# The second layer's setup: bias products between the weight products, and the second half of the tokens normalised among them

## The reference, cut to what matters

```python
x_ln = layernorm(x, ln_g, ln_b)
q = x_flat @ wq + bq
...
v = interp_flat @ wv + bv
k = interp_flat @ wv + bv
...
qh = heads(q @ mq_w + mq_b)
kh = heads(k @ mk_w + mk_b)
vh = heads(v @ mv_w + mv_b)
...
msa = att @ mo_w + mo_b
z = msa + x.reshape(b, h * w, c)
z_ln = layernorm(z, ln_g, ln_b)
out = gelu(z_ln @ mlp_w + mlp_b) + z
```

## Time and profile before

| | us |
|---|---|
| median of 3 runs | 3997.05 |
| lowest and highest run | 3985.2, 4001.21 |
| profiled execution, its own time | 4001.9 |
| its span, first to last instruction | 4000.0 |
| mean granted TensorE clock | 0.983 of full |

### The profile page before, as it was taken

How to read it: one execution, slowest core, us unless ns; L and a number is a source line. 1 busy time by engine, 2 the same in 40 slices (tenths; PEclk the granted TensorE clock), 3 DMA queues, 4 the chain that set the end, 5 groups by cost and what they waited for, 6 DMA issues and landing times. The chain is left out here.

```text
span 4000.0 us, 63404 instructions
## 1 busy us (share of the span) xinstructions
PE 3823.4 (96%) x21614; PEld 3202.0 (80%) x21614; DVE 2958.2 (74%) x5158; ACT 2430.6 (61%) x5241; POOL 1640.5 (41%) x1935
## 2 busy tenths in 40 slices
PE   8999999999999999999999889999999999999999
PEld 6888888888878888878888657777777777777777
DVE  3984984965957938849849647888787888787876
ACT  3873864855847828738648426565556565555656
POOL 1432432433432333324324215554545454555554
PEclk9999999999999999999999989999999999999999
DMA  2231231331331322313312403131313131313221
GB/s 87 54 77 44 63 78 41 66 91 28 61 83 40 60 71 53 75 43 66 76 43 63 135 26 85 64 85 64 85 64 85 64 85 64 85 64 78 71 73 55
DMA packets 175079, 269.31 MB, mean 67 GB/s; under 512 B 58732, under 2 KB 91560, under 8 KB 174760
## 3 DMA queue, kind: packets, MB, share of 16 engines
q1 hardware_dynamic: 170152, 248.48, 25.0%
q0 software_dynamic: 4608, 16.78, 1.3%
HBM read 113.90 MB, written 33.82 MB: 37 GB/s over the span
## 5 line engine op out<-in xcount | busy, mean ns | idle before, releaser
L647 DVE TENSOR_REDUCE a_neg_max<-a_ps 128x1 f32<-128x1024 f32 x512 | 621.9, 1216 | 303.8 <-PE a_ps L481 303.8
L605 ACT ACTIVATE a_ph<-a_ps 128x512 fp32r<-128x512 f32 x1024 | 564.6, 597 | 190.3 <-PE a_ps L495 188.9
L664 DVE TENSOR_TENSOR a_pl<-a_ps,a_ph 128x512 fp32r<-128x512 f32 x1024 | 654.1, 679 | 7.0 <-ACT a_ph L605 3.7
L749 POOL TENSOR_TENSOR a_qk<-a_fold_s,a_fold_r 64x256 f32<-64x256 f32 x256 | 191.7, 749 | 1039.0 <-DVE a_fold_s L655 864.4
L612 ACT ACTIVATE a_prob<-a_ps,a_neg_max 128x1024 f32<-128x1024 f32 x512 | 572.5, 1118 | 31.2 <-DVE a_neg_max L647 31.2
L495 PE MATMUL a_ps<-a_ident,a_prob 128*128 128x128 f32 x4096 | 553.3, 276 | 37.7 <-DVE a_pl L664 36.6
L495 PEld LDWEIGHTS a_ps<-a_ident,a_prob 128*128 128x128 f32 x4096 | 459.8, 140 | 157.4 <-issue 93.8
L510 PE MATMUL a_ps<-a_ph,a_v 128*128 128x256 f32 x2048 | 550.9, 302 | 0.0
L510 PE MATMUL a_ps<-a_pl,a_v 128*128 128x256 f32 x2048 | 509.9, 282 | 0.0
L481 PE MATMUL a_ps<-a_kl,a_qs 128*128 128x512 f32 x1024 | 404.8, 395 | 0.0
L480 PE MATMUL a_ps<-a_kh,a_qs 128*128 128x512 f32 x1024 | 403.1, 394 | 0.0
(11 more groups left out here) (262 smaller groups left out, 9228.4 us busy)
## 6 DMA issues: line engine op xcount, KB each, us to landing
a_qs<-a_qk SPq DMA_DIRECT2D x128, 256.0 KB, 4.3
a_kl<-a_qk SPq DMA_DIRECT2D x128, 256.0 KB, 4.8
a_xtok<-in_x SPq DMA_DIRECT2D x64, 256.0 KB, 4.9
a_fold_r<-a_inv_row SPq DMA_DIRECT2D x256, 64.0 KB, 3.3
b_xs<-x SPq DMA_DIRECT2D x64, 256.0 KB, 4.6
b_qs<-b_qh SPq DMA_DIRECT2D x64, 256.0 KB, 3.1
b_qs<-b_ql SPq DMA_DIRECT2D x64, 256.0 KB, 3.8
b_z<-x SPq DMA_DIRECT2D x64, 256.0 KB, 3.7
```

Of the source, the lines that this page charges most:

```text
L605: act.activation(ph[:, b % 2, 4 * g:4 * g + 4, (u % 2) * P:(u % 2 + 1) * P], ps[:, 4 + n % 2, :].rearrange("p (k q) -> p k q", k=4), ACT.C ...
L647: dve.tensor_reduce(neg_max[:, i_:i_ + 1], ps[:, 2 * (i_ % 2):2 * (i_ % 2) + 2, :] .rearrange("p a b -> p (a b)"), AX, ALU.max, negate=Tru ...
L664: dve.tensor_tensor(pl[here], ps[:, 4 + n % 2, :].rearrange("p (k q) -> p k q", k=4), raw(ph[here]), ALU.subtract).then_inc(pl_ok, 1)
```

## The change

```diff
-        raws = {n: ... for n in ("mq", "mk", "mv", "mo", "wq", "wv", "mlp")}
+        raws = {n: ... for n in ("mlp", "mk", "mv", "mo", "wq", "wv", "mq")}
...
+            FUSE_BANK = (0, 1, 2, 3, 4, 6, 7)
+            BIAS_AT = (0, 4, 4)
... ACT, in the loop over the 12 products
-                    act.activation(wh[n][:, j, :], ps[:, g % 8, :], ACT.Copy).then_inc(hi_ok, 1)
+                    act.activation(wh[n][:, j, :], ps[:, FUSE_BANK[g % 7], :], ACT.Copy).then_inc(hi_ok, 1)
+                    if g == 5:
+                        for t in range(4, TT):
+                            act.wait_ge(ln_ok, t + 1)
+                            high(act, t).then_inc(xh_ok, 1)
... and behind the loop
-                for t in range(4, TT):
-                    act.wait_ge(ln_ok, t + 1)
-                    high(act, t).then_inc(xh_ok, 1)
... PE
-                    if g >= 8:
-                        pe.wait_ge(lo_ok, g - 7)
+                    if g >= 7:
+                        pe.wait_ge(lo_ok, g - 6)
                     for k in range(CT):
-                        mm = pe.matmul(ps[:, g % 8, :], wt[:, k, j * P:(j + 1) * P], raws[m][:, k, :],
+                        pe.matmul(ps[:, FUSE_BANK[g % 7], :], wt[:, k, j * P:(j + 1) * P], raws[m][:, k, :],
+                                  start=k == 0, stop=k == CT - 1)
+                        mm = pe.matmul(ps[:, 5, g:g + 1], raws[m][:, k, j * P:(j + 1) * P],
+                                       vec[:, BIAS_AT[g // 4] + k:BIAS_AT[g // 4] + k + 1],
                                        start=k == 0, stop=k == CT - 1)
                     mm.then_inc(pe_s, 1)
 
-                pe.wait_ge(lo_ok, 10)
+                pe.wait_ge(lo_ok, 9)
...
                 pe.wait_ge(lo_ok, 12)
-                for g, (at, m) in enumerate(((0, "mq"), (4, "mk"), (4, "mv"))):
-                    for j in range(CT):
-                        for k in range(CT):
-                            mm = pe.matmul(ps[:, 5, 4 * g + j:4 * g + j + 1], raws[m][:, k, j * P:(j + 1) * P],
-                                           vec[:, at + k:at + k + 1], start=k == 0, stop=k == CT - 1)
-                mm.then_inc(pe_s, 1)
... DVE, in the loop over the 12 products
+                    if g == 4:
+                        dve.wait_ge(rstd_ok, 2)
+                        dve.wait_ge(pe_s, 13)
+                        for t in range(4, TT):
+                            prepared(dve, t, t + 1)
+                    if g == 6:
+                        for t in range(4, TT):
+                            dve.wait_ge(xh_ok, t + 1)
+                            low(dve, t).then_inc(xl_ok, 1)
... and at the end of its list
-                dve.wait_ge(rstd_ok, 2)
-                for t in range(4, TT):
-                    prepared(dve, t, t + 1)
-                for t in range(4, TT):
-                    dve.wait_ge(xh_ok, t + 1)
-                    low(dve, t).then_inc(xl_ok, 1)
```

More of the change, by code:

```diff
@@ L924, in layer1 @@
         W = Region(nc, q_at, SB_END)
-        raws = {n: W.take(f"b_{n}_raw", [P, CT, C]) for n in ("mq", "mk", "mv", "mo", "wq", "wv", "mlp")}
+        raws = {n: W.take(f"b_{n}_raw", [P, CT, C]) for n in ("mlp", "mk", "mv", "mo", "wq", "wv", "mq")}
         wqt = W.take("b_wq_t", [P, CT, C])
@@ L1148, in _ @@
                     dve.wait_ge(hi_ok, 1 + g + 1)
-                    dve.tensor_tensor(wl[n][:, j, :], ps[:, g % 8, :], raw(wh[n][:, j, :]), ALU.subtract)\
+                    dve.tensor_tensor(wl[n][:, j, :], ps[:, FUSE_BANK[g % 7], :], raw(wh[n][:, j, :]), ALU.subtract)\
                        .then_inc(lo_ok, 1)
+                    if g == 4:
[7 more added lines that the diff above has]
+                            low(dve, t).then_inc(xl_ok, 1)
                     if g == 3:
@@ L1162, in _ @@
                 dve.tensor_scalar(refs[:], refs[:], -1.0, None, ALU.add).then_inc(chn, 1)
-                dve.wait_ge(pe_s, 22)
+                dve.wait_ge(pe_s, 21)
                 for g, (dst, at) in enumerate(((bqm, 8), (bkm, 12), (bvm, 16))):
@@ L1168, in _ @@
                 dve.tensor_copy(wide[:, 1], vec[:, 36:40].unsqueeze(2).to_broadcast([P, CT, P])).then_inc(chn, 1)
-                dve.wait_ge(pe_s, 23)
+                dve.wait_ge(pe_s, 22)
                 dve.tensor_copy(ref[:], ps[:, 4, :].rearrange("p (c s n) -> p c s n", c=2, s=KT)[:, :, :, 0])\
                    .then_inc(chn, 1)
-                dve.wait_ge(pe_s, 24)
+                dve.wait_ge(pe_s, 23)
                 dve.tensor_tensor(bmo[:], ps[:, 2, :], bo_raw[:], ALU.add).then_inc(chn, 1)
                 dve.tensor_tensor(bmlp[:], ps[:, 3, :], bm_raw[:], ALU.add).then_inc(chn, 1)
-                dve.wait_ge(rstd_ok, 2)
-                for t in range(4, TT):
-                    prepared(dve, t, t + 1)
-                for t in range(4, TT):
-                    dve.wait_ge(xh_ok, t + 1)
-                    low(dve, t).then_inc(xl_ok, 1)
         nc.all_engine_barrier()
```

## The result

| | before | changed |
|---|---|---|
| median, us (7 runs each) | 3998.78 | 3979.94 |
| lowest and highest | 3985.2, 4002.9 | 3974.54, 3985.13 |
| profiled execution, its span | 4001.9, 4000.0 | 3974.67, 3972.9 |

A forecast was written before the change was run, and what follows sets the result against it. PE's list, then DVE's tail, was taken to bound the setup. Savings of 5.2, 0.3, 0.8, 2.1 and 8.2 us sum to 16.6, taking the median from 3997.05 to about 3980.5 us; range 3967 to 3994.

The forecast's parts named there:

- loop, first weight load to the projection's: PE's fused loop with the bias products added: 43.23 us before, plus 11.1, so 54.3 us.
- bias matmul between long ones: In PE's fused loop, each bias matmul pair costs two exposed weight loads: 0.23 us, 11.1 us for 48.
- transposes and wide products to DVE's start: PE behind the projection, now at full clock: transposes 0.7 us to their end, then 7.1; savings 0.8 and 2.1.
- from `b_bmo` to POOL (before 10.10): DVE's tail at the setup's end: the second half of the tokens leaves it, 8.2 us saved.
- block of `centre` and `scale` on DVE: Moved token work, 5.8 us, placed in the fused loop where DVE waited for products, from 2320.8 to 2326.6.
- sum: All setup savings together: bias products 5.2, junction 0.3, transposes 0.8, wide products 2.1, tokens 8.2; -16.6 us.
- two bounds of the prediction: Cost of the bias products in PE's loop: at least 5.5 us (chance 8%), at most 20.5 us (chance 10%).
- 11 us of slack: Before the projection: DVE reaches the low part of g = 8 by about 2336, PE needs it at 2346.9.
- the chain passes beside it, so I give nothing: Behind the barrier: PE's first projection finds a higher clock, but POOL's clearings and DVE's convolution bypass it; no gain.
- the falling clock: In the mixed fused loop, bias matmuls' empty stretches bring PE to 1.2 GHz: loop +49 us, 4029 us, chance 4%.
- the stretch of the first layer with 74 weight loads: Evidence against a clock fall: PE holds 1.00 there with 74 loads in 10 us, most exposed between short matmuls.
- the rival: PE's clock falls to half in the mixed fused loop: 103 us against 54.3, kernel 4029 us, chance 4%.

The follow-up runs named there:

- doubled: Against the changed kernel, each bias matmul issued twice, the second into a spare bank with its result unused: setup 103.89 us, time 3994.99 us.
- The kernel with the bias products alone: Against the changed kernel, the second half of the tokens put back at the end of the setup: setup 101.24 us, ratio to before 0.9983.
- The kernel that clears early: Against the changed kernel, POOL clears `b_qpad` inside the setup, wide products between the projection's halves: first load to first convolution 95.60 us, time 3963.79 us.
- the fourfold one: Against the changed kernel, each bias matmul issued four times throughout the loop: setup 204.21 us, time 4078.84 us.

## Why the prediction was right

By its own steps, from the loop's first weight load on (2292.60 before, 2292.10 in the changed kernel, so its clock times stand 0.5 us early):

| step | predicted | measured |
|---|---|---|
| loop, first weight load to the projection's | 54.3 | 2346.64 - 2292.10 = 54.5 |
| bias matmul between long ones | 0.23 | 0.22 (0.22 when doubled) |
| projection | 11.1 | 11.09 |
| transposes and wide products to DVE's start | 7.8 | 2365.47 - 2357.73 = 7.74 |
| from `b_bmo` to POOL (before 10.10) | 8.2 less | 1.90, 8.2 less |
| block of `centre` and `scale` on DVE | 2320.8 to 2326.6 | 2320.20 to about 2326 |
| low part of g = 8 done | 2336 | 2335.2 |
| sum | -16.6 | -16.39 |

*The dearest unknown was the pair* of weight loads that a bias matmul takes. No row of before had one. The value was built from exposed weight loads: a load hides under a long matmul and not under a one-column one. The loads of the changed kernel show just this, 0.11 us from load to load where no long matmul streams (2298.94 to 2299.05, and again to the second of the two loads in that row) and 0.43 where one does (2299.59 to 2300.02). Two of each make the 1.08. Doubling the matmuls gave the same price again. The two bounds of the prediction, one load a pair (5.5 us) and half clock (20.5 us), were both far off.

*The tokens hid.* Their room was read from the rows as 11 us of slack, and 11.4 is there. The kernel with the bias products alone prices it at 10.11 - 1.90 = 8.2 us, with 8.2 predicted.

*Behind the barrier nothing came back.* PE's first projection there now runs at 1.00 (last window above) and not at 0.50, and clearing to convolution is as long as before. The step "the chain passes beside it, so I give nothing" held. The kernel that clears early shows what that stretch did hide: once the clearings are gone the convolution comes 3.8 us sooner, not 6.8.

*Where the argument was weaker than its result.* Against the falling clock I had put that it "held for 4.5 us of nothing but one-column matmuls". That is thin support: three blocks of 16 such matmuls in this very loop brought it down each time, sooner than in 4.5 us, at 10.2 us for the three. The other support, the stretch of the first layer with 74 weight loads, is no such case: its matmuls have 128 and 256 columns and not one, as in this row:

```profile
1400.93 0.28 PE L510 MATMUL a_ps<-a_ph,a_v 128*128 128x256 f32 x1
```

So the moved products are cheap because each stands between long ones, and not because they are in the loop. The other part of the argument, that each is followed by a long matmul, is the one that carried. What the rival really had to fear I had not named: the mixture has to let the clock rise from the cold start. With one or two bias matmuls a place it rises, with four it doesn't, and at half clock through the loop the rival's own sum, +49 us, would have stood. So a loop of this kind can run at half clock throughout. That one matmul a place is on the safe side had no row behind it, and there the forecast had some luck: the argument for 4% did not reach that far. The rule of the Trainium skill (TensorE: Matmul & The Clock Gate, "A second HAM failure mode: psum-queue depth-cycling") tells of a clock that swings where PE goes round the PSUM banks and pauses shortly between groups of matmuls. The prediction held this rule against the loop, but its condition isn't met here: PE is busy for all of the 49.14 us on seven banks, at 1.00. So no run here shows whether it holds.

*The size in the runs.* The 17.6 us of the ratio, with an interval of 13 to 22, agree with the 16.4 of the setup; nothing more need be explained. In the pair of profiles 0.7 us more is the earlier arrival of `mq`, and 10.2 us lie behind the setup.

## What to carry to other kernels

Spread short matmuls singly among long ones at full clock, and look at what the clock did before and behind every block of them; put no block of short ones among them, not even a filler where the clock has just come up. At the end of a setup, ask of each engine what it still does behind the last wait: here half of the gain was DVE work that had idle room 50 us earlier. A setup of under 3% of the time had 28 us in it (conv 116.41 to 88.32), and the order of loads and the clearings behind the barrier, which no busy share shows, gave nearly two thirds as much as the change did.

## What the runs showed of the hardware that I had not expected

*What the clock does depends on where it starts.* The same mixture (one long fp32 matmul, four of one column) stays at 0.50 when it begins there, for 163 us, and holds 1.00 for 55 us when it begins there. At half clock the mixture also takes 3.41 us a place and at full clock 1.75, so that half as many columns are streamed in a microsecond; whether the clock's earlier level itself matters or only the slower stream that comes of it, these runs don't tell. Each of the two is one execution. Blocks of 16 one-column matmuls, with PE busy throughout, end at half clock (the means of the two shown are 0.81 and 0.78), and some 5 us of long matmuls behind them run at 0.50. Where between two and four a place the mixture no longer rises wasn't tried.

*The scatter of the runs is clock.* The stretch behind the first convolution is the same program in 11 of the 13 profiled executions (in the other two a part of its work has moved ahead of it), and lasts 1591.6 to 1609.0 us. I summed the time at half clock in it, over 160 equal windows, each as 2 x (1 - PEclk) x its length: 33.5 to 67.8 us. Before has 67.8 us of it and lasts 1609.0, the changed kernel 47.2 and 1598.8, the fourfold one 33.5 and 1592.9. The correlation over all 13 is 0.94 and the slope 0.47 (0.93 and 0.46 over the 11), so a microsecond at half clock costs about half of itself. By that slope the 20.6 us more of it in before are 9.7 of the 10.2 us by which the first pair of profiles differ outside the setup. The runs without a profile point the same way: of the 13 of before beside the kernel with the bias products alone, the slowest (3999.33) has a mean clock of 0.983 and the three fastest (3985.37 to 3988.26) 0.987. What decides in an execution how long the clock stays low there is open.
